# The order of VectorE's steps within a slot: selections and low parts of messages first

## The reference, cut to what matters

```
xn = layernorm(x)
x  = x + gnn(xn) + mix(xn)
x  = x + moe(layernorm(x))
gnn: out[n] = sum over the edges e into n of (xn[src_e] @ Wr[rel_e]) * norm_e      (100000 edges, 16 relations)
mix: q, k, v = xn @ Wqkv;  k = softmax over the nodes;  o = q @ (k^T v) by head
     gate = sigmoid(gelu(xn' @ Wg1 + bg1) @ Wg2 + bg2);  (o * gate) @ Wproj + bproj
moe: 8 experts, the best 2 of a token by the router's logits;  y_e = gelu(t @ w1[e] + b1[e]) @ w2[e] + b2[e]
     out = t + sum over e of combine[:, e] * y_e
```

## Time and profile before

| | |
|---|---|
| median of 3 runs | 1862.65 us (1862.06 to 1864.38) |
| the profiled execution | 1848.56 us, its span 1847.0 us |
| mean granted clock of TensorE | 0.97 |
| PE busy | 1726.4 us (93%) |
| weight loads (PEld) | 1526.2 us (83%) |
| VectorE busy | 1352.7 us (73%) |
| ScalarE busy | 958.0 us (52%) |
| GpSimd busy | 1005.4 us (54%) |

### The profile page before, as it was taken

One profiled execution on the slowest core, in us unless ns is written; L12 is line 12 of the kernel. 1 busy time (PEld: TensorE's weight loads), 2 busy tenths in 40 slices (PEclk: granted clock), 3 DMA queues, 4 the chain that ended last, 5 costly groups with the idle time before them and its releaser, 6 DMA issues.

```text
span 1847.0 us, 38898 instructions
## 1 busy us (share of the span) xinstructions
PE 1726.4 (93%) x10903; PEld 1526.2 (83%) x10903; DVE 1352.7 (73%) x3331; ACT 958.0 (52%) x2190; POOL 1005.4 (54%) x1132
## 2 busy tenths in 40 slices
PE   4999999989999999996679999999999999999998
PEld 3788888877778777775569999999999999999998
DVE  5767554466667666764678888888888888888885
ACT  3444222344444444443456666666666666666654
POOL 2233222577777777763366665656565656565630
PEclk9999999999999999997779999999999999999999
DMA  6565564566667666668633232333233333233320
GB/s 201 202 229 214 223 234 189 211 218 218 230 208 240 215 221 225 227 215 297 213 104 103 90 97 87 102 89 97 87 102 89 98 88 100 89 99 90 99 58 12
DMA packets 106583, 286.92 MB, mean 155 GB/s; under 512 B 19719, under 2 KB 41052, under 8 KB 93986
## 3 DMA queue, kind: packets, MB, share of 16 engines
q1 hardware_dynamic: 57762, 166.68, 24.3%
q0 software_dynamic: 40032, 110.39, 21.1%
q10 hardware_dynamic: 8736, 9.20, 1.6%
HBM read 148.88 MB, written 137.32 MB: 155 GB/s over the span
## 4 chain that ended last, share of the span: by engine, by line
PE 81%; issue 6%; DVE 5%; ACT 3%; ACTq 1%; another core or an unknown queue 1%; DMA 1%; DVEq 1%; POOL 0%; SPq 0%; POOLq 0%
PE bank L1524 65%; PE bank L1645 3%; PE bank L1646 2%; PE bank L1564 2%; PE bank L1565 2%; ACT mh L892 2%; PE bank L1706 1%; PE bank L1666 1%; DMA slot<-kv_d 1%; PE bank L1618 1%; ACTq L743 1%; DVE xtp L1372 1%; ACT raw L939 1%; PE bank L1681 1%
## 5 line engine op out<-in xcount | busy, mean ns | idle before, releaser
L709 POOL DMA_INDIRECT stg<-table,idxcur x495 | 507.6, 1025 | 375.6 <-PE bank L1646 189.8
L1524 PE MATMUL bank<-wreg,xt 128*128 128x512 f32 x2352 | 594.8, 404 | 13.6 <-issue 13.2
L1524 PEld LDWEIGHTS bank<-wreg,xt 128*128 128x128 f32 x2352 | 442.2, 193 | 114.0 <-issue 18.8
L609 POOL DMA_INDIRECT raw<-table,idxa x297 | 322.0, 1084 | 119.4 <-issue 72.4
L1524 PE MATMUL bank<-tt,wreg 128*128 128x256 f32 (+1 forms) x2400 | 320.6, 283 | 0.3 <-DVE tt L1398 0.3
L1524 PE MATMUL bank<-wreg,ht 128*128 128x256 f32 x2352 | 319.1, 284 | 0.0
L1524 PEld LDWEIGHTS bank<-tt,wreg 128*128 128x128 f32 x2400 | 298.3, 189 | 8.9 <-issue 6.8
L1524 PEld LDWEIGHTS bank<-wreg,ht 128*128 128x128 f32 x2352 | 294.7, 188 | 8.3 <-issue 8.3
L939 ACT ACTIVATE raw<-bank,cols 128x256 f32<-128x256 f32 (+1 forms) x400 | 163.8, 460 | 195.3 <-PE bank L1524 150.0
L1061 DVE COPY stg<-bank 128x512 f32<-128x512 f32 x196 | 133.9, 685 | 157.3 <-PE bank L1524 132.1
L1332 DVE SCALAR_TENSOR_TENSOR ml<-stg,nrm,mh 128x256 fp32r<-128x256 f32 x495 | 214.7, 480 | 36.7 <-ACT mh L892 33.3
(11 more groups left out here) (188 smaller groups left out, 2118.2 us busy)
## 6 DMA issues: line engine op xcount, KB each, us to landing
table<-stg SPq DMA_DIRECT2D x98, 1024.0 KB
kv_d<-kvs SPq DMA_DIRECT2D x49, 257.0 KB
slot<-kv_d SPq DMA_DIRECT2D x49, 257.0 KB
xt_d<-xt SPq DMA_DIRECT2D x49, 256.0 KB
xtp<-xt_d SPq DMA_DIRECT2D x24, 512.0 KB
stg<-table,idxcur POOLq DMA_INDIRECT x495
xres<-in_x POOLq DMA_DIRECT2D x24, 256.0 KB, 3.2
out_x<-xres SPq DMA_DIRECT2D x24, 256.0 KB
```

The costliest lines, as they stand in the source:

```text
L609: pool.indirect_dma_start(ring_a[:, r * EARLY + j, :], None, table[0:LIMIT, :], bass.IndirectOffsetOnAxis(ap=idxa[:, at:at + 1], axis=0)). ...
L709: pool.indirect_dma_start(stg[:, (s % 4) * SUP + j, :], None, table, bass.IndirectOffsetOnAxis(ap=idxcur[:, at:at + 1], axis=0)).then_inc( ...
L1524: mm = pe.matmul(dst, stat(a, c), mov(b, c), start=(n == 0), stop=(n == 3 * chunks - 1))
```

## The change

In the table of slots, SELECT and MSGS now stand first in every slot, ahead of ADD, LOW, TURN_LOW and COMBT_ACT. In slot 0 MSGS moves ahead of LOW 1. WEIGHT of slot 0 stays in front; it is ScalarE's. Since ScalarE reads the same table, its MSGS of slot 3 now comes ahead of COMBT_ACT; nothing else of its order changes. Of PE's steps none changes place against another, and GpSimd and SyncE don't use the table.

```diff
--- before.py
+++ after.py
@@ -1767,18 +1767,18 @@
 
 
 SLOTS_OF_PAIR = (
-    ("-WEIGHT", "*SELECT", "-LOW 1", "*MSGS", "*WINDOW", "-COMB", "-LAYER1 2", "-LAYER2 0", "*SUMS", "+OUT",
+    ("-WEIGHT", "*SELECT", "*MSGS", "-LOW 1", "*WINDOW", "-COMB", "-LAYER1 2", "-LAYER2 0", "*SUMS", "+OUT",
      "+GATES"),
-    ("*SELECT", "-ADD 0", "-LOW 2", "*MSGS", "+GATE_ACT", "+GATE", "-LAYER1 3", "-LAYER2 1", "+GATE_HI", "*SUMS"),
-    ("-ADD 1", "*SELECT", "-LOW 3", "*MSGS", "+GATE_LOW", "*WINDOW", "-LAYER1 4", "-LAYER2 2", "*SUMS", "+PROJ",
+    ("*SELECT", "*MSGS", "-ADD 0", "-LOW 2", "+GATE_ACT", "+GATE", "-LAYER1 3", "-LAYER2 1", "+GATE_HI", "*SUMS"),
+    ("*SELECT", "*MSGS", "-ADD 1", "-LOW 3", "+GATE_LOW", "*WINDOW", "-LAYER1 4", "-LAYER2 2", "*SUMS", "+PROJ",
      "-COMBT"),
-    ("-ADD 2", "*SELECT", "-LOW 4", "-COMBT_ACT", "*MSGS", "+STATS", "-LAYER1 5", "-LAYER2 3", "*SUMS"),
-    ("-ADD 3", "*SELECT", "-LOW 5", "*MSGS", "+MEAN", "*WINDOW", "-LAYER1 6", "+NORM", "-LAYER2 4", "*SUMS"),
-    ("-ADD 4", "*SELECT", "-LOW 6", "*MSGS", "*LAST_WINDOW", "-LAYER1 7", "+TURN", "+TURN_HI", "-LAYER2 5", "*SUMS",
+    ("*SELECT", "*MSGS", "-ADD 2", "-LOW 4", "-COMBT_ACT", "+STATS", "-LAYER1 5", "-LAYER2 3", "*SUMS"),
+    ("*SELECT", "*MSGS", "-ADD 3", "-LOW 5", "+MEAN", "*WINDOW", "-LAYER1 6", "+NORM", "-LAYER2 4", "*SUMS"),
+    ("*SELECT", "*MSGS", "-ADD 4", "-LOW 6", "*LAST_WINDOW", "-LAYER1 7", "+TURN", "+TURN_HI", "-LAYER2 5", "*SUMS",
      "-BIAS2"),
-    ("-ADD 5", "*SELECT", "+TURN_LOW", "-LOW 7", "*MSGS", "-BIAS2_ADD", "*WINDOW", "-LAYER2 6", "+LAYER1 0",
+    ("*SELECT", "*MSGS", "-ADD 5", "+TURN_LOW", "-LOW 7", "-BIAS2_ADD", "*WINDOW", "-LAYER2 6", "+LAYER1 0",
      "+LOGIT", "*SUMS"),
-    ("-ADD 6", "*SELECT", "+LOW 0", "*MSGS", "+TOP", "-LAYER2 7", "+LAYER1 1", "-ADD 7", "*SUMS"),
+    ("*SELECT", "*MSGS", "-ADD 6", "+LOW 0", "+TOP", "-LAYER2 7", "+LAYER1 1", "-ADD 7", "*SUMS"),
 )
```

## The result

| | before | after |
|---|---|---|
| median | 1863.52 us (1862.06 to 1866.85, 4 runs) | 2035.43 us (2026.40 to 2041.73, 4 runs) |
| profiled execution, span | 1848.56, 1847.0 us | 2032.1, 2030.6 us |
| mean granted clock | 0.97 | 0.934 |
| PE busy | 1726.4 us (93%) | 1797.7 us (89%) |
| VectorE busy | 1352.7 us (73%) | 1350.3 us (66%) |

The ratio is 1.0916, 95% interval 1.0868 to 1.0964: slower, as forecast, but by 172 us where the forecast was 71. The time is outside its range of 1897 to 1968.

A forecast was written before the change was run, and what follows sets the result against it. PE was taken as the bound (81% of the chain of waits). (1.39 + 1.70) x 22 = 68.0, plus 1.4 and 2, gave 71.4 us on 1848.56: 1920; with 14.1 for the median, 1934 us, range 1897 to 1968.

The forecast's parts named there:

- slots 3 to 6: Low parts and ADD 5 ahead of TURN_LOW make the next pair's LAYER1 0 start 1.70 us later a turn.
- the sum: Both chains' losses over 22 turns plus the edge pairs: 71.4 us added, nothing for the clock.
- Slot 2: End of the gate: ADD 1 and LOW 3 run between low parts and GATE_LOW, so PROJ starts 1.39 us later a turn.
- one-chain rival: Only one of the two chains, to PROJ or to LAYER1 0, loses: 1892 us; chance 0.10.
- second rival: The clock falls to half after slot 2 in many turns, adding 9 to 37 us: 1943 to 1971; chance 0.17.
- The rest, nothing: All steps moved outside slot 2 and slots 3 to 6 cost nothing, having slack or only moving idle time.
- No change: VectorE's 5.2 us of idle time a turn swallows what is moved: 1862.65 us; chance 0.03.
- faster: Earlier low parts give PE back 0.46 us a turn in slot 4, 10 us in all: 1852; chance 0.05.

The follow-up runs named there:

- e7: Kernel before with only the rows of slots 2 and 6 in the new order: 1840.96 us, ratio 1.0368.
- e1: Kernel before with only slot 2 in the new order: 1799.35 us, ratio 1.0131.
- e2: Kernel before with only slot 6 in the new order: 1815.46 us, ratio 1.0215.
- e10: Kernel before with three extra ScalarE copies between the GELU and the cast of expert 7 in each turn: 1801.0 us, ratio 1.0139.
- e9: Changed kernel with three extra ScalarE copies between the GELU and the cast of expert 7 in each turn, quick chip: 1952.88 us, ratio 1.1013.
- f4: The changed kernel itself, run again on a slow chip: 2033.25 us, ratio 1.0909.
- e3: Changed kernel with slot 6 put back as before: 1812.04 us, ratio 1.0207.
- e6: The changed kernel itself, run again on a quick chip: 1841.85 us, ratio 1.0379.
- e8: Against the changed kernel: slots 0, 1, 5 to 7 as before, slot 2's GATE_LOW ahead of the low parts, slot 4's MEAN ahead of LOW 5: 1765.80 us, ratio 0.9953.
- f5: Changed kernel with 24 unneeded PE products ahead of LAYER1 0's wait for `tt`, quick chip: 1867.34 us, ratio 1.0510.
- f6: Changed kernel with TURN_LOW as the first step of slot 6, quick chip: 1805.27 us, ratio 1.0168.
- f1: Changed kernel with three extra ScalarE copies ahead of the cast of expert 7, slow chip: 2093.63 us, ratio 1.1230.
- f2: Kernel of f1 with 24 unneeded PE products ahead of LAYER1 0's wait for `tt`, same chip: 2046.04 us, ratio 1.0964.
- e5: The kernel before, unchanged, run again on a quick chip for its trace: 1777.8 us, one execution.
- e11: Changed kernel with six extra ScalarE copies between the GELU and the cast of expert 7 in each turn: 2023.85 us, ratio 1.1408.

## Why the prediction was right in direction and wrong in size

The step that failed is the price of LAYER1 0's wait in slots 3 to 6, 1.70 us a turn. It held nothing for a late release of PE, and the sum held nothing for the clock. On the first chip the release added 2.1 us a turn to the wait, and the falls of the clock at that wait 2.8 us a turn more.

**Slot 2, +1.39 us a turn.** Right in mechanism. VectorE idles before the low parts, then ADD 1 and LOW 3 stand between them and GATE_LOW; PROJ waits 1.5 us for `xtp` on the first chip. On a quick chip the part costs 24.7 us for 22 turns, 1.1 a turn.

**Slots 3 to 6, +1.70 us a turn. This is the step that failed.** Its queue was right: three low parts and ADD 5 ahead of TURN_LOW, no cover left, and a quick chip charges 1.6 to 1.9 a turn for it (e7's cost less e1's: 41.0 us; e2: 40.8). But I took ScalarE's rows of slots 4 to 6 and moved them by 0.29 us. On the first chip the cast of expert 7 moved by 2.3 us more, because the release of expert 5's second layer came late. I had seen such a release in the earlier trace rows (2.69 us of idle time ahead of GELU 3) and used it only as an argument that an order might be shifted, in the one-chain rival. The release that hurt was itself on time in every turn of the trace before, so that trace could tell that releases come late, but not that this one would. A term was due all the same: a chain that had 0.97 us of cover and now has none takes any lateness in full. e10 and e9 show the difference, 1.07 against 1.93 us of the same delay.

**The clock.** It was my second rival at 0.17, with 9 to 37 us, put behind slot 2, and the sum had it at nothing. It fell in 21 of 22 turns, at LAYER1 0's wait. In slot 2, where I had looked for the thin stretch because the earlier trace rows resembled it, hardly anything came: e1 has that slot's new order and a clock of 1.00 in its turns, and in f4 one spell of the loop stands there. On the first chip the turns average 44.6 us and the one without a fall takes 41.8: 2.8 us a turn, some 62 us in all. The price of 1.7 us for 3.3 us at half clock was right: the turns with one such spell (3.4 us) take 1.7 us more than the one without. Wrong was the length, mostly 6.8 us and in five turns 10.2 (which cost 4.1 in e9), and that I didn't look at the standstill that my own sum made.

**The sum.** On quick chips the change costs 66.6 us, 3.8%; the sum was 71.4 us. On slow chips: 67 us of order, about 46 us of late release (41.8 less 36.9 less 2.8 a turn, 22 turns), some 62 us of clock, together 175 for the 172 measured. The first of these terms is the quick chips', and no run measured it on a slow one.

**The range.** Its upper end, 1968, was called the middle of the clock case, but that case ran from 1943 to 1971, with its middle at 1957. The measured 2035 lies beyond either.

**The rest, nothing.** Right within 12.7 us (e1 against e3), and within 0.9 us beside the two big terms (e6 against e7).

**The other rivals.** Only one chain loses: no, each costs by itself (e1, e2), and together they add up (e7). No change and faster: wrong for this order. The attack on late low parts does pay where nothing that PE awaits stands behind them: e8, 0.5% and 1.0%.

**Open.** What makes PE's releases come late on some chips, and why the new order moves the lateness to expert 5's second layer. It comes at the same products in turn after turn of one kernel, but no run varied the lateness of the release itself, only that of the cast. What filling or shortening the standstill does to the changed kernel on a slow chip was not measured either (f5 and f6 came on a quick one); there the clock's part rests on f1 and f2.

## What to carry to other kernels

In an in-order queue, put first what the bounding engine awaits, and let work that waits for a third engine stand behind it. Where a moved step has used up its cover, price it with the largest lateness that the trace shows at any release, also where this one was on time, and not with the place of the rows alone. When the sum leaves the bounding engine a standstill of a few microseconds in each turn, charge the clock to it as well, and compare the order on more than one chip.

## What the runs showed of the hardware that I had not expected

- The same kernel takes 1775 to 1777 us on four chips and 1861 to 1865 us on three, at a clock of 0.98 and 0.97.
- On the slow ones a release from PE can reach ScalarE 2.5 to 2.6 us after the products' modelled end (22 turns of 22 in the changed kernel, and again in f4); the same release was on time in the kernel before on the first chip. On the quick ones (e5, e6) no ScalarE wait for an unnamed release is left.
- PE's standstill of 1.3 us a turn left the clock at full (2.4 GHz, e6); 3.3 us dropped it to half (1.2 GHz) in two of three turns, for 10.2 us each (e9); 5.2 us (e11) in each turn, for 3.4 to 13.7 us. 2.5 us of standstill behind a filler (f2) still went with a fall in 12 of 22 turns.
- What a spell at half clock costs went with its length: 3.4 us cost 1.4 to 1.7 us (f2, first chip), 10.2 us cost 4.1 us (e9).
